# Row sums of an attention softmax: five pairs of probability tiles added by accumulating transfers instead of three tiles summed on TensorE

## The reference, cut to what matters

```python
q = rotary_pos_emb(q); k = rotary_pos_emb(k)          # 16 heads of 32
logits = jnp.einsum('bhik,bhjk->bhij', q, k)
a = jax.nn.softmax(logits, axis=-1)                   # over 2048 keys
y = jnp.einsum('bhij,bhjv->bhiv', a, v)
```

## Time and profile before

| | |
|---|---|
| median of 3 runs | 4029.58 us (4029.5 to 4034.14) |
| profiled execution | 4030.17 us, span of its instructions 4028.5 us |
| attention, first to last copy of values (L764) | 513.2 to 2215.7 us, 31 blocks apart |
| TensorE busy, share of the span | 89% |
| GpSimd busy, share of the span | 57% |
| mean granted TensorE clock | 0.943 |

### The profile page before, as it was taken

The page is one execution under the profiler, slowest core; times in us unless marked ns, Lnnn a source line. Parts: engine busy times, 40 slices in busy tenths (PEclk is TensorE's granted clock), DMA queues, the critical chain, the costliest instruction groups (busy, mean ns, idle before and its releaser), DMA issues. The chain is left out here.

```text
span 4028.5 us, 50249 instructions
## 1 busy us (share of the span) xinstructions
PE 3595.8 (89%) x17632; PEld 2341.1 (58%) x17632; DVE 2031.7 (50%) x3302; ACT 1588.7 (39%) x2895; POOL 2282.0 (57%) x1776
## 2 busy tenths in 40 slices
PE   7996999999999999999999344999899957996998
PEld 6774445545544454444453333888688845875776
DVE  5652877767777677767773334111111133332333
ACT  3331366656666566666666113111111122221232
POOL 3555499979999799989999211222122232442443
PEclk9998799999999999999999677999899978997999
DMA  5546513103140304122100555011101121011010
GB/s 204 164 146 150 78 22 54 32 21 55 22 64 22 65 16 60 22 44 42 22 4 7 168 191 192 19 45 43 64 21 43 53 102 47 32 40 55 25 44 21
DMA packets 114748, 253.88 MB, mean 63 GB/s; under 512 B 12672, under 2 KB 13184, under 8 KB 108160
## 3 DMA queue, kind: packets, MB, share of 16 engines
q1 hardware_dynamic: 114496, 250.64, 23.9%
HBM read 155.17 MB, written 95.16 MB: 62 GB/s over the span
## 5 line engine op out<-in xcount | busy, mean ns | idle before, releaser
L714 DVE TENSOR_REDUCE part_max<-ps_att 128x1 f32<-128x512 f32 x2048 | 1271.7, 683 | 484.6 <-PE ps_att L633 484.3
L800 POOL TENSOR_TENSOR prob_sums<-prob_sums,probs 128x512 f32<-128x512 f32 x1152 | 1433.6, 1284 | 75.4 <-ACT probs L757 75.4
L757 ACT ACTIVATE probs<-ps_att 128x512 f32<-128x512 f32 x2048 | 1060.3, 603 | 585.0 <-PE ps_att L603 569.7
L603 PE MATMUL ps_att<-q_stack,k_stack 97*128 97x512 f32 x2048 | 867.4, 427 | 26.9 <-PEq L49 21.1
L633 PE MATMUL ps_att<-k_stack,q_stack 96*128 96x512 f32 x2048 | 831.6, 413 | 41.6 <-DMA k_stack<-qk 41.2
L603 PEld LDWEIGHTS ps_att<-q_stack,k_stack 97*128 97x128 f32 x2048 | 390.1, 191 | 503.6 <-ACT probs L757 286.7
L655 PE MATMUL ps_att<-probs,v_tok 128*32 128x512 f32 x4096 | 545.5, 605 | 0.0
L1247 POOL TENSOR_TENSOR ml_g_lo<-ml_g,ml_g_hi 128x512 fp32r<-128x512 f32 x128 | 164.8, 1287 | 649.0 <-DVE ml_g_hi L1223 649.0
L633 PEld LDWEIGHTS ps_att<-k_stack,q_stack 96*128 96x128 f32 x2048 | 400.2, 196 | 135.8 <-DMA k_stack<-qk 41.6
L1223 DVE CAST ml_g_hi<-ml_g 128x512 fp32r<-128x512 f32 x128 | 54.7, 427 | 571.8 <-ACT ml_g L1183 571.8
L1183 ACT ACTIVATE ml_g<-ps_mlp 128x512 f32<-128x512 f32 x128 | 76.5, 598 | 585.6 <-PE ps_mlp L1262 585.6
(11 more groups left out here) (192 smaller groups left out, 4765.6 us busy)
## 6 DMA issues: line engine op xcount, KB each, us to landing
q_stack<-qk SPq DMA_DIRECT2D x192, 128.0 KB, 4.4
k_stack<-qk SPq DMA_DIRECT2D x48, 512.0 KB, 19.4
qk<-rot_hi SPq DMA_DIRECT2D x64, 256.0 KB, 4.9
qk<-rot_lo SPq DMA_DIRECT2D x64, 256.0 KB, 3.2
x_in_sb<-in_x SPq DMA_DIRECT2D x8, 1024.0 KB, 8.4
v<-v_stage SPq DMA_DIRECT2D x8, 1024.0 KB, 4.4
v_tok<-v SPq DMA_DIRECT2D x8, 1024.0 KB, 32.0
yT<-o_sb SPq DMA_DIRECT2D x32, 256.0 KB, 2.5
```

The costliest lines, as they stand in the source:

```text
L603: nc.tensor.matmul(sT[u % 3], t["kS"][0:S3 + 1, b, h, k * P:(k + 1) * P], t["qS"][0:S3 + 1, h, n * TB:(n + 1) * TB], start=True, stop=True)\
L714: nc.vector.tensor_reduce(t["pm"][:, r, k:k + 1], mx[mx_uses % 3], AX.X, ALU.max)\
L757: nc.scalar.activation(t["p"][:, at % PR, h, :], sT[(at * G + h) % 3], ACT.Exp)\
L800: nc.gpsimd.tensor_tensor(x, first, t["p"][:, at % PR, h, :], ALU.add).then_inc(s["acc_done"], 1)
```

## The change

Only the tiles of steps 8 and 14 are still summed on PE. Five pairs of neighbouring tiles, (0,1), (3,4), (6,7), (9,10), (12,13), are first added in place by a transfer issued from GpSimd's queue with an addition at its destination: `probs[k] += probs[k+1]`, 1 MB each. It waits for the exponentials of step k+1 and for the product of tile k with v. GpSimd then has nine operands in place of eleven (the sums of the pairs and the tiles 2, 5, 11, 15), and so eight rounds of four additions. `POOL_ROUNDS` lists them as (step at which the round stands in GpSimd's program, tile added): the last two stand at steps 16 and 18, which are steps 0 and 2 of the next block. `LAST_AT` goes from 4 to 5. Both tiles of a pair come free when the round that takes the pair's sum has run. At the end of each group GpSimd issues a `dma_reset`.

```diff
-PE_SUMS = (6, 8, 10, 12, 14)
-POOL_SUMS = tuple(k for k in range(LT) if k not in PE_SUMS)
-POOL_ADDS = G * (len(POOL_SUMS) - 1)
-LAST_AT = 4
+PE_SUMS = (8, 14)
+PAIRS = (0, 3, 6, 9, 12)
+POOL_FIRST = 2
+POOL_ROUNDS = ((5, 0), (7, 5), (9, 3), (11, 6), (12, 11), (14, 9), (16, 15), (18, 12))
+POOL_ADDS = G * len(POOL_ROUNDS)
+LAST_AT = 5
...
-        k = max(w % LT, POOL_SUMS[1])
-        return w // LT * POOL_ADDS + G * (POOL_SUMS.index(k) - 1) + h + 1
+        k = w % LT - (w % LT - 1 in PAIRS)
+        r = 0 if k == POOL_FIRST else [x for _, x in POOL_ROUNDS].index(k)
+        return w // LT * POOL_ADDS + G * r + h + 1
+
+    def pair_sem(n, k):
+        m = n * len(PAIRS) + PAIRS.index(k)
+        return s[f"paired{m % 2}"], 16 * (m // 2 + 1)
...
-            for at in range(end):
-                n, k = at // LT, at % LT
-                for h in range(G if k in POOL_SUMS[1:] else 0):
-                    pool.wait_ge(s["exp"], at * G + h + 1)
+            def add_pair(n, k):
+                w = n * LT + k
+                pool.wait_ge(s["exp"], G * (w + 2))
+                pool.wait_ge(s["pv"], w + 1)
+                sem, value = pair_sem(n, k)
+                nc.gpsimd.dma_start(t["p"][:, w % PR], t["p"][:, (w + 1) % PR], accum_op=ALU.add).then_inc(sem, 16)
+
+            def add_round(n, r):
+                k = POOL_ROUNDS[r][1]
+                w = n * LT + k
+                if k in PAIRS:
+                    sem, value = pair_sem(n, k)
+                    pool.wait_ge(sem, value)
+                for h in range(G):
+                    pool.wait_ge(s["exp"], w * G + h + 1)
                     x = t["acc"][:, n % 2, h, :]
-                    if k == POOL_SUMS[1]:
+                    if r == 0:
                         if n >= 2:
                             pool.wait_ge(s["sum_done"], n - 1)
-                        first = t["p"][:, POOL_SUMS[0] % PR, h, :]
+                        first = t["p"][:, POOL_FIRST % PR, h, :]
                     else:
-                        pool.wait_ge(s["acc_done"], added(at, h) - G)
+                        pool.wait_ge(s["acc_done"], n * POOL_ADDS + G * (r - 1) + h + 1)
                         first = x
-                    nc.gpsimd.tensor_tensor(x, first, t["p"][:, at % PR, h, :], ALU.add).then_inc(s["acc_done"], 1)
+                    nc.gpsimd.tensor_tensor(x, first, t["p"][:, w % PR, h, :], ALU.add).then_inc(s["acc_done"], 1)
+
+            for at in range(end + LT if attend else 0):
+                n, k = at // LT, at % LT
+                if at < end and k - 2 in PAIRS:
+                    add_pair(n, k - 2)
+                for r, (offset, _) in enumerate(POOL_ROUNDS):
+                    if offset == k and at < end:
+                        add_round(n, r)
+                    if offset == LT + k and n:
+                        add_round(n - 1, r)
+            if attend:
+                nc.gpsimd.dma_reset()
```

More of the change, by code:

```diff
@@ L815, in attention @@
         names = ("q_in0 q_in1 q_in2 q_in3 k_in v_in mx_full mx_free neg_max max_set0 max_set1 score exp pv psum acc_done "
-                 "sum_done o_kept l_kept y_stored l_stored ones_set")
+                 "paired0 paired1 sum_done o_kept l_kept y_stored l_stored ones_set")
         s = phase(nc, ctx, " ".join("at_" + n for n in names.split()))
```

## The result

| | before | after |
|---|---|---|
| median | 4029.81 us (4 runs) | 4077.9 us (4069.82 to 4086.28, 4 runs) |
| ratio, 95% interval | 1 | 1.0121 [1.0105, 1.0137] |
| span of the profiled execution | 4028.5 us | 4077.6 us |
| granted TensorE clock | 0.943 | 0.926 |

The change costs 48 us where 38.6 us less were forecast. The page first: busy time, transfers, and the group of additions.

What follows compares the result with a forecast made beforehand. PE was taken to set the pace, GpSimd following with some 4 us to spare a block. Sums removed -82.6, group ends +32, loads +12 give -38.6 us: 4030.2 to 3992 us, range 3972 to 4060.

Steps and rivals of the forecast that it cites:

- What bounds the kernel, and the price of a sum on PE: In the attention PE sets the pace; a sum costs it 0.86 us, so three fewer save 2.6 us a block.
- Issue and landing: GpSimd's adding transfers of 1 MB: 1.0 us to issue each, 6.9 us to land.
- The loop through GpSimd: Pairs issued behind rounds that wait for earlier pairs: 46.8 us a block, under 51.7, so PE still sets the pace.
- Rivals A and C: A: the transfer is slow by itself, 4170 us, chance 0.15. C: GpSimd becomes the bound through issues, 4065, chance 0.07.
- C's "about +35": Cost if issues take 2.5 us each: GpSimd's sum 52.3 us, ends and loads 10 more each time; 4065 us.
- The ends of groups: Three rounds follow pair 12's issue with nothing to cover them: 8.1 us at each of four ends, +32.
- "The k and v loads", +12 us: Pairs meeting the loads in seven halves land after 11 to 16 us; 1.8 us lost a half.
- Its end at 16 us: Upper landing beside the loads: eight load pieces' turns with the transfer's own time on top; 4 us a half.
- the prediction's own figures for other landings: Loss a half by landing time beside the loads: 4 us at 16, 16 us when pairs wait some 30.
- rival B: Loads hold pairs 0 and 6 up some 30 us, 16 us lost in seven halves: 4092 us, chance 0.06.
- By that rule alone I had worked out 4008 us: Engines alternating between queues packet by packet give the 16 us landing: +28 in place of +12, 4008 us.

Runs made afterwards that it cites:

- run 1: The changed kernel with the k and v loads inside the attention cut to 32 columns each, full tiles loaded once before: 3982.5 us, 0.9882.
- run 3: The changed kernel, but in each group's last block PE sums tile 15 and the pair 12 itself: 4046.9 us, 1.0036.
- run 6: The changed kernel with the k and v loads in one piece, issued at step 6 of the half instead of its start: 4086.1 us, 1.0139.
- run 4: The changed kernel with k loaded in 24 transfers of 128 KB with 2 KB pieces, in place of six of 512 KB: 4052.3 us, 1.0053.
- run 8: The changed kernel with loads one at a time, k away from the query loads, and PE summing tiles 8, 12 to 15 in each group's last block: 3946.3 us.
- run 5: The changed kernel with whole k and v transfers one at a time, k from step 2 to 22, v at 26: 4015.7 us, 0.9964.
- run 7: The changed kernel with the loads of run 5, and PE summing tiles 8, 12 to 15 in each group's last block: 3982.6 us, 0.9875.

## Why the prediction was wrong

**What bounds the kernel, and the price of a sum on PE: right.** The block is 51.7 us, 2.6 less.

**Issue and landing: right.** 0.96 us against 1.0, though GpSimd's next instruction starts 0.6 us after the issue; 7.6 against 6.9. The estimate worked out from the Trainium skill for the landing (Collectives: The Full Stack, "Why ReduceScatter is half of AllGather") had been 6.2 us; the measurement decides, and lies over both.

**The loop through GpSimd: right.** 30 + 2.9 + 2 x 7.6 = 48 us, under 51.7; outside the loads ACT hardly waits (18 us in all in run 1). Rivals A and C did not come. C's "about +35" does not follow from its own parts: 32 x (52.3 - 54.25) + 32 + 12 = -18, and 10 more at each of 11 places gives +92.

**The ends of groups: right in mechanism, sized 32 us, measured 36.** The meeting of the engines hides none of it, as run 3 shows.

**"The k and v loads", +12 us: this step failed; it is 92 to 95 us.** Its end at 16 us took the transfer as it is shared out once it runs: eight of its pieces, a load piece between each two. That part held: from its first packet on, pair 0 took 14 to 16 us in the seven halves (940 to 956 above). What it left out is that the transfer first got nothing for 11 us. By the prediction's own figures for other landings (4 us a half at 16, 16 at 30) one of 27 gives some 13 us a half; 13 were measured, where 1.8 had been put in. I had a row that showed such a delay, a store that needed 28.7 us behind the loads, and set it aside because it was in the loads' own queue. That was the error of judgement: rival B, priced with exactly this row (landing 30, 16 us a half, 4092 us), had its mechanism and nearly its size, 27 us and 13 us a half, and got a chance of 0.06.

What the runs show in its place: a pair issued while the six k transfers and v are outstanding waits 11 us for its first packet, whether it is the first or the third pair of the half (run 6), mostly less when the loads come in short pieces and are issued over 21 us (5 to 11 us, run 4), and at most 5.6 us when they come one at a time and mostly apart from others (run 8; run 5 still had them meet the query loads). Behind one k transfer or v alone it waits no more than 2.7 us (run 5). That the engines have taken up load work ahead, and finish it before they look at the other queue, fits these runs, but no run looks into an engine, so it is argued and not shown. Nor does any run separate the number of outstanding transfers from their going into 16 partitions only, so how much each contributes stays open. The Trainium skill (DMA: Bandwidth & Descriptors, "Queues, rings and completion order") says that an engine goes round its queues packet by packet. If its packet is taken as one packet of the profile, the traces agree from the first one on, and do not agree before it. By that rule alone I had worked out 4008 us.

**The clock** was no term of mine. Of the 11.2 us that the block of 63 us loses, 8.6 are PE idle and 2.7 are the same matmuls run partly at the 1.2 GHz level after it.

## What to carry to other kernels

A transfer that the pace depends on has to be priced by the queue work that is outstanding when it is issued, on every queue, not by bandwidth; a bulk load that was hidden before may be the thing it meets. Issue hidden bulk loads one transfer at a time, apart from other loads and spread up to the step that needs them, as soon as a transfer with a deadline shares the engines. And look for a row that already shows the bad case: if its reason for being different is only that it sat in another queue, give it weight.

Work moved to a slower path should be moved back where nothing follows: the ends of groups paid 9.4 us (the last 7.5) for rounds that made the last block 1.7 us longer when PE did their sums (51.2 us in run 7 against 49.5 in run 5).

## What was not expected of the hardware

- No packet for 11 us, then turns of one for one, for a transfer issued from GpSimd's queue behind six 512 KB loads with 8 KB pieces into 16 partitions each and one of 1 MB; 5 to 11 us with pieces of 2 KB for the six.
- About as short a wait behind one load alone, 2.6 us behind 512 KB into 16 partitions and 2.1 behind 1 MB into 128, each issued under 2 us before.
- GpSimd's additions are recorded as 1618 ns each instead of 1285 ns, but their rate is unchanged: at a group's end twelve take 15.24 us, 1.27 each. The longer records are no loss:

```profile
895.73 15.24 POOL L820 TENSOR_TENSOR prob_sums<-prob_sums,probs 128x512 f32<-128x512 f32 x12
```
- A transfer of 1 MB with an addition from one part of the on-chip memory to another lands in 7.3 us at the median with the loads made small, and GpSimd is free for its next instruction about 0.6 us after the issue began (549.19 to 549.79).
